# Self-attention mask applied by VectorE, ScalarE and GpSimd instead of by two mask matmuls per group of four heads

## What is computed

```python
wei = jnp.einsum('bhtd,bhsd->bhts', q, k) * scale
causal = jnp.tril(jnp.ones((T, T), bool))
wei = jnp.where(causal[None, None], wei, NEG_INF)
wei = jnp.where(tgt_padding_mask[:, None, None, :], NEG_INF, wei)
wei = jax.nn.softmax(wei, axis=-1)
sa_out = _merge(jnp.einsum('bhts,bhsd->bhtd', wei, v)) @ sa_wproj + sa_bproj
```

## Time and profile before

| what | value |
|---|---|
| median of 3 runs | 696.6 us (696.01 to 700.79) |
| the profiled execution's own time | 695.2 us |
| its span (first to last instruction) | 693.5 us |
| what lies around the span | 1.7 us |
| mean granted TensorE clock | 0.942 |
| instructions | 14116 |
| HBM read, written | 14.36 MB, 1.84 MB |

### The profile page before, as it was taken

How to read it: one execution, slowest core, us unless ns; L and a number is a source line. 1 busy time by engine, 2 the same in 40 slices (tenths; PEclk the granted TensorE clock), 3 DMA queues, 4 the chain that set the end, 5 groups by cost and what they waited for, 6 DMA issues and landing times.

```text
span 693.5 us, 14116 instructions
## 1 busy us (share of the span) xinstructions
PE 598.6 (86%) x5564; PEld 454.6 (66%) x5564; DVE 415.2 (60%) x982; ACT 326.6 (47%) x613; POOL 128.0 (18%) x370
## 2 busy tenths in 40 slices
PE   3587897997989998897989998797979999998696
PEld 3475675665767776675757776575767677766564
DVE  5983564695447644696547644686537654684471
ACT  3124343454535654345634655245634655374154
POOL 6602311021002211012002211112002211130010
PEclk9968997998989999999999999999999999999898
DMA  7292058192760049293671039194671048204700
GB/s 237 77 128 66 1 98 134 41 125 35 106 109 21 11 86 139 39 122 43 101 107 36 5 92 142 38 113 48 97 109 42 1 87 125 36 1 96 88 6 14
DMA packets 73121, 52.07 MB, mean 75 GB/s; under 512 B 21920, under 2 KB 72288, under 8 KB 73056
## 3 DMA queue, kind: packets, MB, share of 16 engines
q1 hardware_dynamic: 73056, 51.17, 46.2%
HBM read 14.36 MB, written 1.84 MB: 23 GB/s over the span
## 4 chain that ended last, share of the span: by engine, by line
PE 44%; SPq 14%; DMA 12%; DVE 9%; ACT 7%; issue 3%; POOL 1%; DVEq 0%; POOLq 0%; ACTq 0%
SPq L525 14%; PE misc L1058 7%; PE pvb L1029 6%; PE scb L1013 5%; PE misc L918 5%; PE mxb L997 5%; DMA k2st<-kp 4%; DMA k1st<-kp 4%; DMA tb<-in_x 4%; PE misc L920 3%; PE misc L919 3%; PE misc L1065 3%; DVE rem L764 3%; DVE negm L830 2%; ACT prob L701 2%
## 5 line engine op out<-in xcount | busy, mean ns | idle before, releaser
L701 ACT ACTIVATE prob<-scb 125x448 f32<-125x448 f32 (+1 forms) x256 | 137.2, 542 | 77.7 <-PE scb L1013 72.1
L830 DVE TENSOR_REDUCE negm<-mxb 112x1 f32<-112x375 f32 x256 | 130.1, 539 | 22.9 <-PE mxb L997 21.0
L1029 PE MATMUL pvb<-prob,v 125*17 125x112 f32 (+1 forms) x2048 | 97.5, 269 | 0.3 <-ACT ot L708 0.3
L997 PE MATMUL mxb<-k2st,q2st 96*112 96x375 bf16 x256 | 85.4, 349 | 2.4 <-DVE negm L830 1.6
L1013 PE MATMUL scb<-q2st,k2st 128*125 128x112 bf16 x768 | 79.0, 226 | 0.2
L1013 PEld LDWEIGHTS scb<-q2st,k2st 128*125 128x125 bf16 x768 | 67.7, 139 | 15.7 <-issue 7.6
L827 DVE TENSOR_REDUCE negm<-mxb 112x4 f32<-112x448 f32 x64 | 39.6, 619 | 61.7 <-PE mxb L994 61.4
L620 POOL CAST mparts<-negm 112x8 bf16<-112x8 f32 x64 | 12.1, 189 | 346.9 <-DVE negm L830 173.6
L1058 PE MATMUL misc<-wf,hT 128*112 128x256 f32 x256 | 60.4, 384 | 3.2 <-DVE rem L764 3.2
L1029 PEld LDWEIGHTS pvb<-prob,v 125*17 125x17 f32 (+1 forms) x2048 | 35.1, 96 | 36.3 <-issue 21.7
L1058 PEld LDWEIGHTS misc<-wf,hT 128*112 128x112 f32 x256 | 44.7, 179 | 14.7 <-DVE rem L764 4.7
(11 more groups left out here) (153 smaller groups left out, 1261.4 us busy)
## 6 DMA issues: line engine op xcount, KB each, us to landing
k2st<-kp SPq DMA_DIRECT2D x192, 93.8 KB, 4.5
xs<-in_ctx SPq DMA_DIRECT2D x16, 375.0 KB
q1st<-qp SPq DMA_DIRECT2D x48, 112.0 KB, 4.8
k1st<-kp SPq DMA_DIRECT2D x48, 112.0 KB, 7.7
q2st<-qp SPq DMA_DIRECT2D x96, 56.0 KB, 2.3
xn<-in_x SPq DMA_DIRECT2D x4, 448.0 KB, 11.3
tb<-in_x SPq DMA_DIRECT2D x8, 224.0 KB, 10.0
out<-ostage SPq DMA_DIRECT2D x16, 112.0 KB, 3.5
```

The costliest lines, as they stand in the source:

```text
L701: nc.scalar.activation(prob[0:rows, n % PROB_SLOTS, :], scb[n % SCORE_BANKS][0:rows, 0:GH * T], ACT.Exp, scale=SCALE).then_inc(s_ex, 1)
L830: V.tensor_reduce(negm[:, at, i:i + 1], mx[0:T, 0:S], axis=AX_X, op=ALU.max, negate=True).then_inc(s_mx, 1)
L997: mm = M(mx[0:T, 0:S], q2st[0:NROW, i, b * T:(b + 1) * T], k2st[k2_place(q, b)][0:NROW, i, 0:S], start=True, stop=True)
L1029: mm = M(pvb[32 * j:32 * j + VW, g * T:(g + 1) * T], vals, prob[0:rows, slot, j * T:(j + 1) * T], start=(c == 0), stop=(c == chunks(u) - 1))
```

## The change

The two mask matmuls per group of four heads are gone, on the side of the maxima and on the side of the scores; four score matmuls now each start and stop by themselves.

- Maxima: VectorE does four `tensor_tensor_reduce` per group in place of one TENSOR_REDUCE: each negates 112 scores of one head, adds the (now positive) mask and takes the minimum into `negm`; it also writes its full result, back into the PSUM bank. `max` waits for the mask by itself, on VectorE.
- Padding in the scores: ScalarE's exponential gets `pad` as its bias, one value per key row.
- Causality in the scores: GpSimd clears later keys in the probabilities of four heads (`affine_select`, in place, 112x448 f32) behind each exponential, and `pv` waits for this (`s_sel`) in place of the exponential.
- The mask tile is made by one SCALAR_TENSOR_TENSOR per group from a new tile `padrow`, the mask bytes spread over all partitions; its DMA is issued in the start-up behind that of `mask8`, and `s_vec` is waited for at 144 in place of 128.

```diff
             sp.dma_start(mask8[:, :].bitcast(U32), maskT).then_inc(s_vec, 16)
+            sp.dma_start(padrow[:, :, :].rearrange("p t b -> p (t b)").bitcast(U32),
+                         maskT.rearrange("(a t) n -> a (t n)", a=1).broadcast_to([T, T * B // 4])).then_inc(s_vec, 16)
...
             nc.gpsimd.affine_select(out=causal[:, :], in_=causal[:, :], compare_op=ALU.is_ge, fill=MASKED,
-                                    base=0, pattern=[[1, T]], channel_multiplier=-1).then_inc(s_const, 1)
+                                    base=0, pattern=[[-1, T]], channel_multiplier=1).then_inc(s_const, 1)
...
+                elif kind == "score" and s[2] < BG:
+
+                    after(pool, s_ex, s)
+                    p = prob[0:T, scores.index(s) % PROB_SLOTS, :].rearrange("p (h t) -> p h t", h=GH)
+                    nc.gpsimd.affine_select(out=p, in_=p, compare_op=ALU.is_ge, fill=0.0,
+                                            base=0, pattern=[[0, GH], [1, T]], channel_multiplier=-1).then_inc(s_sel, 1)
...
+                    bias = pad[:, q * BG + s[2]:q * BG + s[2] + 1] if s[2] < BG else 0.0
                     nc.scalar.activation(prob[0:rows, n % PROB_SLOTS, :], scb[n % SCORE_BANKS][0:rows, 0:GH * T], ACT.Exp,
-                                         scale=SCALE).then_inc(s_ex, 1)
+                                         bias=bias, scale=SCALE).then_inc(s_ex, 1)
...
-            act.wait_ge(s_vec, 128)
+            act.wait_ge(s_vec, 144)
...
                 if kind == "mask":
-                    V.tensor_copy(padneg[:, :], pad[:, q * BG:(q + 1) * BG]).then_inc(s_pad, 1)
-                    after(dve, s_pad, s)
-                    after(dve, s_sc, ("score", q - 1, BG - 1, 3, 0) if q else None)
-                    for b in range(BG):
-                        i = V.tensor_scalar(maskt[:, b, :], causal[:, :], padneg[:, b:b + 1], None, ALU.add)
-                    i.then_inc(s_mask, 1)
+                    after(dve, s_mx, ("max", q - 1, BG - 1, 3) if q else None)
+                    V.scalar_tensor_tensor(maskt[:, :, :], padrow[:, :, q * BG:(q + 1) * BG].rearrange("p t b -> p b t"), MASKED,
+                                           causal[:, :].unsqueeze(1).broadcast_to([T, BG, T]), ALU.mult, ALU.add).then_inc(s_mask, 1)
...
-                        V.tensor_reduce(negm[:, at, i * GH:(i + 1) * GH], mx[0:T, 0:GH * T].rearrange("p (h s) -> p h s", h=GH),
-                                        axis=AX_X, op=ALU.max, negate=True).then_inc(s_mx, 1)
+
+                        after(dve, s_mask, ("mask", q))
+                        for j in range(GH):
+                            own = mx[0:T, j * T:(j + 1) * T]
+                            one = V.tensor_tensor_reduce(own, own, maskt[:, u, :], -1.0, -MASKED, ALU.add, ALU.min,
+                                                         negm[:, at, i * GH + j:i * GH + j + 1])
+                        one.then_inc(s_mx, 1)
...
                     if i == 0 and u < BG:
-                        after(pe, s_mask, ("mask", q))
                         after(pe, s_q1st, ("stack_q1", q))
...
                     if u < BG:
-                        M(mx[0:T, 0:GH * T].rearrange("p (h s) -> p h s", h=GH), maskt[:, b, :],
-                          identb[0:T, :].unsqueeze(1).broadcast_to([T, GH, T]), start=True, stop=False)
                         for j in range(GH):
                             h = i * GH + j
                             mm = M(mx[0:T, j * T:(j + 1) * T], q1st[0:NROW, h, b * T:(b + 1) * T], k1st[0:NROW, h, b * T:(b + 1) * T],
-                                   start=False, stop=(j == GH - 1))
+                                   start=True, stop=True)
...
-                    if u < BG:
-                        M(sc[0:T, 0:GH * T].rearrange("p (h t) -> p h t", h=GH), identb[0:T, :],
-                          maskt[:, b, :].unsqueeze(1).broadcast_to([T, GH, T]), start=True, stop=False)
...
-                    after(pe, s_ex, ("score", q, u, g, c))
+                    after(pe, s_sel if u < BG else s_ex, ("score", q, u, g, c))
```

More of the change, by code:

```diff
@@ L310, in layer_kernel @@
         pad = sb("pad", [T, B])
-        padneg = sb("padneg", [T, BG])
         maskt = sb("maskt", [T, BG, T], BF16)
+        padrow = sb("padrow", [T, T, B], U8)
         negm = sb("negm", [T, 2, H])
@@ L373, in layer_kernel @@
         s_xs = [sem(f"src_landed{i}") for i in range(2)]
-        s_pad = sem("pad_terms_made")
+        s_sel = sem("later_keys_cleared")
         s_mask = sem("mask_tile_made")
@@ L432, in layer_kernel @@
         signalled(s_resb, od.of("norm2"))
-        for s in (s_pad, s_mask):
-            signalled(s, od.of("mask"))
+        signalled(s_mask, od.of("mask"))
+        signalled(s_sel, [t for t in scores if t[2] < BG])
         for b in range(BG):
@@ L729, in _ @@
             act.wait_ge(s_bcol, 3)
+            act.wait_ge(s_init, 5)
             run()
@@ L862, in _ @@
             V.tensor_copy(identb[0:T, :], ident[0:T, 0:T]).then_inc(s_init, 1)
-            dve.wait_ge(s_vec, 128)
+            dve.wait_ge(s_vec, 144)
             def lo_of(n):
@@ L1012, in pe_part @@
                         ks = k1st[:, h, b * T:(b + 1) * T] if u < BG else k2st[k2_place(q, b)][:, h, c * SC:(c + 1) * SC]
-                        mm = M(sc[0:rows, j * T:(j + 1) * T], ks, (q1st if u < BG else q2st)[:, h, b * T:(b + 1) * T], start=(u >= BG), stop=(u >= BG or j == GH - 1))
+                        mm = M(sc[0:rows, j * T:(j + 1) * T], ks, (q1st if u < BG else q2st)[:, h, b * T:(b + 1) * T], start=True, stop=True)
                     mm.then_inc(s_sc, 1)
@@ L1072, in bias_columns @@
                 return mm
-            pe.wait_ge(s_vec, 128)
+            pe.wait_ge(s_vec, 144)
             pe.wait_ge(s_w[0], 16)
```

## The result

The changed kernel takes 703.9 us (median of 15 executions, 699.6 to 709.0), the kernel before beside it 699.2 us (15 executions). The ratio is 1.0087, 95% interval 1.0059 to 1.0114: slower, and within the 1% that the forecast calls no change. The medians are of all executions, while the ratios leave out disturbed ones, so the two differ: here they give 4.7 and 6.1 us. The profiled execution took 706.0 us with a span of 704.3, against 695.2 and 693.5 before. Those 10.8 us are more than both, because the profile of before is of an execution 4 us under its kernel's median and the one of after of an execution 2 us over its own.

A forecast was written before the change was run, and what follows sets the result against it. PE was the largest part of the chain that ended last (44%), with slack in roughly half the time. Terms -8.5 + 2.6 + 1.0 + 4.8 + 0.5 + 0.3 = +0.7 us gave 697 us, range 686 to 709.

The forecast's parts named there:

- no change: The whole kernel: the forecast's main case, 697 us, within about 1% of before; own range 690 to 703, chance 0.46.
- Mask matmuls, -8.5 us: On PE: the removed mask matmuls give back two thirds of the chain's 12.8 us; bounds -5 and -12.8.
- VectorE, +2.6 and +1.0: Maxima on VectorE: pairs of 0.30 us, mostly hidden, cost +2.6 us over 3.5 periods and +1.0 in the first group.
- GpSimd, +4.8 and +0.5: Selects on GpSimd: behind the residual's DMA wait +2.4 us in two periods, +4.8; in the first group +0.5.
- First group and start-up, +1.0, +0.5, +0.3: First group: VectorE's last-group latency +1.0 us, selects with little room +0.5; start-up: the new DMA +0.3, at most +2.
- ScalarE's bias, 0: ScalarE's exponential: the bias is an operand of the same instruction and costs 0.
- PE's time comes back: Rival, faster: all 12.8 us of PE's chain return and the residual costs 1.2 us twice; 688 us, chance 0.24.
- the serial pair: Rival, slower: on VectorE each pair takes 0.43 us without overlap; +8.7 us, 705 us, chance 0.19.
- GpSimd's queue holds PE: Rival, slower: the residual stall costs its whole 4.5 us in all four groups; +13.6 us, 710 us, chance 0.11.

The follow-up runs named there:

- f1: e3 with 128 matmuls that do no work, of the old mask matmul's size, in all the old places; 706.4 us, ratio to before 1.0099.
- e3: The changed kernel with GpSimd's residual add of half 1 moved three quarters later; 699.4 us, ratio to before 0.9984.
- g1: The changed kernel without GpSimd's selects, so no causality in the probabilities; 697.5 us, ratio to before 1.0008.
- e1: The changed kernel with the score mask back on TensorE, no bias and no select; 696.2 us, ratio to before 0.9994.
- f3: The kernel before with GpSimd's residual add moved as in e3; 694.9 us, ratio to before 0.9953.
- g4: The kernel of e1 with the residual add moved as in e3; 692.0 us, ratio to before 0.9909.
- g2: The changed kernel with one reduction per group for the four pairs, no mask in the maxima; 703.7 us, ratio to before 1.0084.
- e4: The changed kernel with 32 matmuls that do no work, in the first group of batches alone; 705.6 us, ratio to before 1.0086.
- f4: e3 with GpSimd's two row statistics operations of the next group moved late, to norm1's place; 707.6 us, ratio to before 1.0123.
- g3: e3 with one select of GpSimd moved ahead of the next group's row statistics; 693.1 us, ratio to before 0.9961.

## Why the prediction was right, and where it wasn't

Forecast +0.7 us in sum, no change; measured +4.7 us by median (+6.1 by the ratio of 1.0087). That is within 1%, at its edge, and in the whole range of 686 to 709 us; but 703.9 us lies outside the 690 to 703 that the forecast of no change had as its own, and nearest to the 705 of a rival whose mechanism the rows refute. That the sum came out near is partly luck: the pairs were booked with 3.6 us that did not come, and the first group with the start-up with 1.8 where its fifth mT came 5.6 us late. The terms:

- **Mask matmuls, -8.5 us.** 128 slots put back cost 7.0 to 8 us (f1 against e3), where 24.3 would be every slot's time and 12.8 the chain's pieces. The size holds, for adding. Taking them away shows less: g1, with all slots gone and no selects, is level with before (697.5 to 697.9 us, ratio 1.0008), and 1.3 us over e1, which keeps the scores' slots and has no bias. Part of the answer is the first group, below. Another is a wait that the forecast named as a reason to take two thirds: PE's waits for VectorE's splits (`rem`) are 24.4 and 24.6 us in the two profiles of before and 26.6 in f3, 24.5 to 24.6 in the changed kernels whose scores keep or get back a 448-column matmul throughout (e1, g4, f1), and 26.2 to 31.5 in the eight without. The pairs are not the reason, since g2 has 28.9 without them. So a part of PE's saved time turned into waiting there.
- **VectorE, +2.6 and +1.0.** The mis-sized term: it measured 0.2 us (g2). The pair was taken at 0.30 us and takes 0.23, and the rest hides in VectorE's idle time. Only in the first group does the profile show it, fifth mT 1.5 us earlier in g2 than in the changed kernel, and that is lost again later.
- **GpSimd, +4.8 and +0.5.** 5.5 to 6.4 measured (g1). The size and the stall held: PE stops at the residual for 4.37 and 5.16 us (4.5 forecast). That a part comes back afterwards shows too: against the first profile of before the mT matmuls are 6.5 us late ahead of the first stall, 10.1 behind it and 7.7 some 45 us later, and 7.1, 10.6 and 7.7 around the second. These profiles don't show that what is left is 2.4 us each. Incomplete was the cause: the row statistics behind the add would have held the same select. The forecast counted their 1.01 us and not their own wait for a DMA.
- **First group and start-up, +1.0, +0.5, +0.3.** This is the step that went wrong most clearly. By the fourth mT the sum is right (1.7 us late), but between the fourth and the fifth another 3.9 us go. All nine profiles of kernels with fewer mask matmuls and no dummies show the fifth mT 3.7 to 6.2 us late, mostly at a clock of 0.50 in these stretches; the three of kernels with all of them show 0 to 0.7. The forecast took the durations at the clock that the profile of before had, and didn't ask whether the removed work was what had raised it. How much of the 3.9 us is the clock alone stays open: with dummies it is 1.0 (f1) and 2.4 us (e4), including the time of the dummies themselves, but it is 2.4 in f4 too, which has no dummies and a clock of 0.50 from 66 to 78 us.
- **ScalarE's bias, 0.** 0.09 us per instruction, 5.8 us of ScalarE in all; the chain that ended last holds three of these 64 (0.63, 0.64 and 0.63 us), so some 0.3 us on it. The Trainium skill (ScalarE: Activation LUTs, What ACT_TABLE_LOAD costs) gives about 93 ns more for each operand that points to a value per partition; the trace agrees, 632 against 542 ns. What the bias costs the whole kernel wasn't run by itself.

The terms can't simply be added, since the price of the dummies and that of the selects each contain a piece of the first group (f1's fifth mT is 2.5 us earlier than e3's, g1's 0.9 us earlier than the changed kernel's). Two steps do it without counting twice. From before to g1, with the slots gone, the pairs and the bias in and the first group slow, it is -0.4 us by median (+0.6 by the ratio); from g1 to the changed kernel, the selects, +6.4 (+5.5). That makes +6.0 (+6.1), against +4.7 (+6.1); the medians' two values of before are 1.3 us apart. In the first step 4.7 us of the first group and 0.2 of the pairs leave some -5 us for the slots, the forecast's bound and not its -8.5. This last is an estimate from one profile, good to 3 us at best, and it takes for granted that the first group's delay is never made up.

The rivals: that PE's time comes back fell, both with the selects' 6 us and with g1, which has no selects and is level with before; the serial pair fell with rows 0.23 us apart; GpSimd's queue holds PE was right in its mechanism (two whole stalls of 4.4 and 5.2 us) and not in its number of four.

## What to carry to other kernels

An engine whose queue is in program order must not get work that is due soon behind a step that waits for a DMA; look there for every such step, since with one moved the next takes its place (e3, then g3), and move it no further than the one instruction that needs to pass (f4). A move that helps the changed kernel has to be tried on the old one before it is booked as the change's price (f3). Ask of removed matmuls whether the clock was at its full level only with them.

## What the runs showed of the hardware

- Two instructions per head on VectorE, of 307 and 142 ns for 112 elements, step at 0.23 us; 256 such pairs cost the kernel nothing measurable.
- A bias per partition makes the 112x448 exponential 90 ns longer (632 against 542 ns).
- GpSimd's select costs 587 ns for 112x448, where the earlier trace rows has 278 ns for 112x112: 0.92 ns for each further element of a row.
- With the mask matmuls of the first group gone, all or half of them, the granted clock stayed at or fell back to 0.50 until about 78 us, where it had been 1.00 from 62 to 74 us, and dummies brought it back to 1.00 at no gain in time. In g2 that was so with PE busy for 3.97 of the 4 us up to 62.
- A scalar_tensor_tensor that reads bytes 16 apart takes 965 ns for 112x448, and nobody waits for it.
